# Input weights from transposes of a weighed table, and a rewritten start-up, in a state-space convolution with routed low-rank FFN

## The reference

```python
dtA = A * dt[:, None];  Cs = Cc * (jnp.exp(dtA) - 1.0) / A
P = dtA[:, :, None] * jnp.arange(length)
K = 2.0 * jnp.einsum('hn,hnl->hl', Cs, jnp.exp(P)).real
y = irfft(rfft(u * mask) * rfft(K)) [:L] + (u * mask) * D;  y = y * mask
logits = einsum('bsd,ed->bse', y, route_w);  topk_v, topk_idx = top_k(logits, 1)
route_weight = one_hot(topk_idx) * topk_v
h = einsum('bsd,erd->bser', y, A);  wh = route_weight[..., None] * h
out = x + einsum('bser,eor->bso', wh, Bw)
```

## Time and profile before

| | |
|---|---|
| three runs | 608.71, 609.56, 609.94 us (median 609.56) |
| the profiled execution | 609.9 us, its span 608.1 us |
| granted TensorE clock | 1.00 over the span |
| busy: PE, DVE, ACT, POOL | 581.6, 490.3, 317.2, 385.9 us |
| instructions in the span | 13318 |

### The profile page before, as it was taken

The page is one execution under the profiler, slowest core; times in us unless marked ns, Lnnn a source line. Parts: engine busy times, 40 slices in busy tenths (PEclk is TensorE's granted clock), DMA queues, the critical chain, the costliest instruction groups (busy, mean ns, idle before and its releaser), DMA issues.

```text
span 608.1 us, 13318 instructions
## 1 busy us (share of the span) xinstructions
PE 581.6 (96%) x3617; PEld 529.0 (87%) x3617; DVE 490.3 (81%) x1371; ACT 317.2 (52%) x1059; POOL 385.9 (63%) x520
## 2 busy tenths in 40 slices
PE   3589999999999999999999999999999999999996
PEld 3478999999999989999999999999999999999984
DVE  7768888887888888788888888888888888887875
ACT  3666754555465455546545554664555456445420
POOL 4668657666765766676575667657566765665430
PEclk9999999999999999999999999999999999999999
DMA  6212454454345344434534443453444345445422
GB/s 119 73 54 86 149 155 98 144 155 125 120 148 156 100 141 153 125 119 148 157 96 143 153 135 110 148 157 97 143 152 132 114 147 157 102 139 151 138 85 83
DMA packets 37582, 77.64 MB, mean 128 GB/s; under 512 B 12476, under 2 KB 20862, under 8 KB 37510
## 3 DMA queue, kind: packets, MB, share of 16 engines
q1 hardware_dynamic: 28358, 43.76, 28.8%
q10 hardware_dynamic: 9152, 33.03, 13.3%
HBM read 43.16 MB, written 33.62 MB: 126 GB/s over the span
## 4 chain that ended last, share of the span: by engine, by line
PE 92%; DVE 3%; ACT 2%; issue 1%; POOL 1%; DMA 0%; ACTq 0%; POOLq 0%
PE psYo L1060 20%; PE psZ L1080 19%; PE psO L1060 15%; PE psYe L1060 13%; PE psS L1060 11%; PE psO L1107 5%; PE psXe L1071 5%; PE psXo L1071 5%; PE psZ L1136 1%; DVE psS L918 0%; DVE ex L758 0%; DMA logs<-in_L_cond_log_dt_dram 0%; POOL both L465 0%; DVE ost L957 0%; ACT L577 0%
## 5 line engine op out<-in xcount | busy, mean ns | idle before, releaser
L504 POOL TENSOR_TENSOR Slo<-Sf,Shi 128x384 fp32r<-128x384 f32 x64 | 65.3, 1021 | 166.1 <-ACT Shi L651 166.1
L918 DVE SCALAR_TENSOR_TENSOR psS<-Sf,tab,psS 64x128 f32<-64x128 f32 x256 | 91.9, 359 | 48.1 <-ACT Sf L646 41.2
L1080 PE MATMUL psZ<-Wt,Y 128*128 128x136 f32 x1024 | 129.2, 279 | 0.0
L1080 PEld LDWEIGHTS psZ<-Wt,Y 128*128 128x128 f32 x1024 | 123.3, 190 | 0.1
L646 ACT ACTIVATE Sf<-psS 128x128 f32<-128x128 f32 x64 | 17.8, 277 | 200.3 <-PE psS L1060 200.3
L957 DVE TENSOR_TENSOR ost<-psO,xt 128x512 f32<-128x512 f32 x128 | 87.7, 690 | 1.2 <-PE psO L1060 1.1
L497 POOL TENSOR_TENSOR Xlo<-xeven,Xhi 128x512 fp32r<-128x512 f32 x64 | 82.9, 1295 | 0.0
L465 POOL TENSOR_TENSOR both<-coarse,fine 128x512 f32<-128x512 f32 x64 | 69.0, 1079 | 1.3 <-ACT fine L591 1.2
L941 DVE TENSOR_TENSOR wlo<-psZ,whi 128x128 fp32r<-128x128 f32 x64 | 18.7, 292 | 41.2 <-ACT whi L656 41.2
L1060 PE MATMUL psYo<-Xhi,Thi 128*128 128x512 f32 x128 | 51.2, 400 | 0.0
L1060 PE MATMUL psYo<-Xlo,Thi 128*128 128x512 f32 x128 | 51.1, 399 | 0.0
(11 more groups left out here) (193 smaller groups left out, 1522.2 us busy)
## 6 DMA issues: line engine op xcount, KB each, us to landing
xt<-in_x_dram SPq DMA_DIRECT2D x64, 512.0 KB, 4.9
out_dram<-ost ACTq DMA_DIRECT2D x63, 512.0 KB, 5.1
Traw<-kdram SPq DMA_DIRECT2D x64, 128.0 KB, 2.9
kdram<-krow SPq DMA_DIRECT2D x64, 1.0 KB
A_nat<-in_L_ffn_A_dram SPq DMA_DIRECT2D x1, 512.0 KB, 5.1
B_nat<-in_L_ffn_Bw_dram SPq DMA_DIRECT2D x8, 64.0 KB, 3.5
out_dram<-ost SPq DMA_DIRECT2D x2, 256.0 KB, 2.0
lens_i<-in_itok_B_dram SPq DMA_DIRECT2D x1, 64.0 KB, 5.0
```

The source lines that it names most:

```text
L504: pool.tensor_tensor(Slo[h.s2][:, :], Sf[h.s2][:, :], Shi[h.s2][:, :].bitcast(F32), ALU.subtract).then_inc(slo_done, 1)
L918: dve.scalar_tensor_tensor(psS[to, new], Sf[h.s2][fr, old], tab2[fr, BR, h.n:h.n + 1], psS[to, new], ALU.mult, ALU.add).then_inc(brought_d ...
L1080: last = pe.matmul(psZ[:, 0:NW], Y[:, j, c, :], Wt[:, 2 * c + j, :], start=(j == 0 and c == 0), stop=(j == 1 and c == NE - 1), skip_group_ ...
```

## The change

The matrix `Mx` and the constant `twin` go. Instead ACT weighs the table itself: `same` is Grev times the column MA of `tab2`, on all 128 partitions, and `cross` is Grev times MB, each half of 64 partitions read from the other half (`cross_parts`). POOL adds the two to `Wg` (`w_table`), and PE turns `Wg` by two transposes into psB. The samples of K come from a row sum of psB that ACT accumulates while it copies (`scrap`, twice), and K(0) with D folded in comes from a fifth column `K0` of the table.

```diff
-            def m_matrix(h):
-                need(act, b_mm, h.n - 1)
-                for j, table in enumerate((M0, M1)):
-                    act.activation(Mx[h.s2][:, j * N:(j + 1) * N], twin[:, j * N:(j + 1) * N], ACT.Copy,
-                                   scale=col(tab2[:, table, :], h)).then_inc(mx_done, 1)
-                act.activation(Mx[h.s2][:, P:P + 1], col(tab2[:, CK, :], h), ACT.Copy).then_inc(mx_done, 1)
+            def cross_parts(h):
+                need(act, grev_done, h.n + 1)
+                need(act, wg_done, h.n)
+                act.activation(same[:, :], Grev[h.s2][:, :], ACT.Copy, scale=col(tab2[:, MA, :], h)).then_inc(crossed, 1)
+                for to, fr in ((slice(0, N), slice(N, P)), (slice(N, P), slice(0, N))):
+                    act.activation(cross[to, :], Grev[h.s2][fr, :], ACT.Copy,
+                                   scale=tab2[fr, MB, h.n:h.n + 1]).then_inc(crossed, 1)
...
-                act.activation(kcol[h.s2][:, 0, 0:1], psB[:, 0, P:P + 1], ACT.Copy).then_inc(kcol_done, 1)
-                act.activation(kcol[h.s2][:, 1, 0:1], psB[:, 1, P:P + 1], ACT.Identity,
-                               bias=Dcol[:, h.n:h.n + 1]).then_inc(kcol_done, 1)
+                need(act, kcol_done, h.n * 3)
+                for j in range(2):
+                    act.activation(scrap[:, j, :], psB[:, j, 0:N], ACT.Copy,
+                                   accum_out=kcol[h.s2][:, j, 0:1]).then_inc(kcol_done, 1)
+                act.activation(kcol[h.s2][:, 2, 0:1], col(tab2[:, K0, :], h), ACT.Copy).then_inc(kcol_done, 1)
...
+            def w_table(h):
+                need(pool, crossed, h.n * 3 + 3)
+                need(pool, b_mm, h.n - 1)
+                pool.tensor_tensor(Wg[h.s2][:, :], same[:, :], cross[:, :], ALU.add).then_inc(wg_done, 1)
...
-                    last = pe.matmul(psB[:, j, :], Grev[h.s2][:, j * P:(j + 1) * P],
-                                     Mx[h.s2][:, :], start=True, stop=True, skip_group_check=True)
+                    last = pe.transpose(psB[:, j, :], Wg[h.s2][:, j * P:(j + 1) * P], ident[:, :])
```

```diff
             def step(head):
...
-                if head(3).there:
-                    m_matrix(head(3))
                 if head(1).there:
                     x_hi(head(1), 0)
                     x_hi(head(1), 1)
+                if is_head(head(0), 1):
+                    b_hi(head(1))
                 if head(2).there:
                     b_hi(head(2))
...
                 if head(3).there and not is_head(head(0), 1):
                     g_hi(head(3))
+                    cross_parts(head(3))
+                if head(-1).there:
+                    w_hi(head(-1))
                 if part_at(head(7)):
                     turns(part_at(head(7)))
                 if part_at(head(4)):
                     mirror(part_at(head(4)))
-                if head(-1).there:
-                    w_hi(head(-1))
-                if head(3).there and is_head(head(0), 1):
+                if is_head(head(0), 1):
+                    mirror(parts[1])
+                    g_hi(head(2))
                     g_hi(head(3))
+                    cross_parts(head(3))
```

```diff
+            def keep_busy(bank_, n):
+                for _ in range(n):
+                    pe.matmul(bank_[:, 0:P], ident[:, :], ident[:, :], start=True, stop=True, skip_group_check=True)
...
+            keep_busy(psO[0], 7)
             inputs(first[0])
+            pe.wait_ge(tab_done, 2)
+            keep_busy(psS, 3)
             bring(first[0])
             turn_x(first[1], 0)
             turn_x(first[1], 1)
             inputs(first[1])
+            pe.wait_ge(blo_set, 2)
+            keep_busy(psY[0], 8)
+            from_states(first[0])
             within(first[0], 0)
             within(first[0], 1)
-            inputs(first[2])
-            from_states(first[0])
             run_steps(step)
```

More of the change, by code:

```diff
@@ L525, in step @@
                     g_lo(head(3))
+                    w_table(head(3))
             first = [Head(n) for n in range(4)]
-            exponents(pool, *RHO_PARTS[0])
             angle_steps(parts[0])
-            x_lo(first[0])
+            angle_steps(parts[1])
             turn_parts(parts[0])
@@ L709, in _, with b_high @@
             mirror(parts[0])
-            act.wait_ge(tabs_turned, 2)
-            act.activation(tab2[:, :, :], psX[0][:, 0:5 * H].rearrange("p (t h) -> p t h", h=H),
-                           ACT.Copy).then_inc(tab_done, 1)
-            act.wait_ge(tab_done, 2)
-            m_matrix(first[0])
-            for j in range(2):
+            def b_high(j):
                 act.wait_ge(b_turned, j + 1)
@@ L726, in _ @@
             b_hi(first[1])
+            s_hi(first[0])
+            x_even(first[1])
+            g_hi(first[1])
             t_hi(first[0])
-            s_hi(first[0])
-            g_hi(first[1])
-            x_even(first[1])
-            turns(parts[1])
-            m_matrix(first[2])
-            b_hi(first[2])
-            g_hi(first[2])
-            sines(parts[1])
-            m_matrix(first[3])
-            t_hi(first[1])
-            g_hi(first[3])
-            mirror(parts[1])
+            sines(parts[1])
+            cross_parts(first[2])
+            t_hi(first[1])
+            g_hi(first[2])
+            cross_parts(first[3])
             run_steps(step)
@@ L964, in step @@
                     x_lo(head(1))
+                if is_head(head(0), 1):
+                    turn_k(head(1))
+                    b_lo(head(1))
                 if head(-1).there:
@@ L1157, in step @@
                     turn_x(head(1), 1)
-                if head(2).there:
+                if is_head(head(0), 1):
+                    inputs(head(1))
+                elif head(2).there:
                     inputs(head(2))
@@ L1161, in step @@
                     project(head(-1))
+                if is_head(head(0), 1):
+                    inputs(head(2))
                 if head(0).there:
```

337 lines of the change are left out of this document (185 added, 152 removed).

## The result

The changed kernel takes 652.10 us (median of 4 runs, 651.65 to 652.22), the kernel before 609.14 us beside it. The ratio is 1.070 (95% interval 1.069 to 1.072). I had forecast 631.6 us and a range up to 641. The direction and the mechanism were right; two terms of the sum were too small, and one was missing. The profiled span is 650.4 us, 42.3 more than before.

What follows compares the result with a forecast made beforehand. PE bounds the kernel before, with ACT's chain 0.15 us behind; the change makes that chain the bound. Span 608.1 + 3.9 (start-up) + 18.6 (58 steps) - 0.5 (end) = 630.1; predicted time 631.6 us, range 612 to 641.

Steps and rivals of the forecast that it cites:

- second to `whi` 0.49 - 0.10 = 0.39: ACT, each step: `whi` starts 0.39 us after the second `cross` starts, with the usual overlap back.
- the sum 1.72 us from `Ghi` to `whi`: ACT, each step: `same` and two `cross` put `whi` at t + 5.59, t being the step's first ACT copy.
- POOL's part: hidden: POOL, each step: `Wg` adds one 734 ns instruction, hidden because PE needs it only at the next step's input weights.
- The start-up's term: Steps before step 3: t (first ACT copy) of step 3 comes 3.9 us later; from 4 us gained to 7 lost.
- the end: Last steps: 0.5 us less, as they have no weighing any more and no two transposes on PE.
- PE's two transposes: PE, each step: the two new transposes take 0.22 us, in place of input weights taking 0.45 us.
- the 8.63 us that PE would need: PE, each step: its own work falls from 8.86 to 8.63 us; 13.3 us less if PE stayed the bound.
- the accumulating copies and `m_matrix`: ACT ahead of `Shi`: added copies hidden, removed `m_matrix` gives nothing back, as ACT waits 0.35 us for DVE there.
- The first: Rival, ACT: copies between halves overlap like any others, only the column costs; 617.6 us in all; chance 0.17.
- The second (faster): Rival: the three ACT instructions take 0.93 us, PE stays the bound; 599.7 us, at best 592; chance 0.14.
- The third (`Shi` late): Rival, ACT: accumulating copies take so long that `Shi` is 0.2 us late or more; 643 us; chance 0.09.
- The fourth: Rival, start-up: the fillers don't raise PE's clock, which moves the time by nothing; no chance given.

Runs made afterwards that it cites:

- experiment 3: Two runs of the changed kernel: each `cross` writing the half it reads (wrong results), 642.44 us; the two `cross` instructions in swapped order, 643.80 us.
- Experiment 2: Kernel before, with `same` and two `cross` computed and thrown away behind `Ghi`, and `whi` behind them, ahead of `turns` and `mirror`: 638.17 us, ratio 1.048.
- Experiment 5: Changed kernel with the work the change had put into step 1 moved back ahead of it on all engines; steps unchanged: 642.67 us, ratio 1.055.
- last run of experiment 9: Changed kernel with only ACT's issue of the output's store moved from ahead of `Sf` to behind `Bhi`: 644.68 us, ratio 1.058.

## Why the prediction was wrong

**The step that failed first** was "second to `whi` 0.49 - 0.10 = 0.39", with the sum 1.72 us from `Ghi` to `whi`. The three instructions take 1.90 us. `Ghi` to `same` (0.31), `same` to `cross` and `cross` to `cross` (0.51 forecast, 0.52 and 0.53) were right in number, though not for the reason that I gave: without the crossing of the halves they are as far apart (experiment 3). The last one to `whi` is 0.53. I took the overlap from the four copies of a mirror, whose last one writes partitions 0 to 63; the last `cross` writes 64 to 127. Swapping the two brought it back (experiment 3). This is 0.14 us a step, and with 0.03 of rounding and of copies a little longer, 0.16 to 0.17, over 58 steps 9.4 us.

**A term that was missing** is the fourth step. "POOL's part: hidden" was true of `Wg` for PE, but `Wg` moves `Grev` 0.7 us on, under which DVE's `frac` is held, ahead of the carry. With the chain through ACT as bound, this costs 0.27 to 0.28 us in 13 steps, 3.6 us. Experiment 2, with the same chain and no `Wg`, doesn't have it. So the 58 steps are 18.6 + 9.4 + 3.6 = 31.6; measured 31.6.

**The start-up's term** was 3.9 us and is 10.2. t of step 1 is 43.50 and not 41.9: the first input weights start at 24.90 and not near 23.5, head 0's `Slo` at 31.37 and not near 30, and the rest is as long as I said (ACT's 2.59 us of waiting for the table of head 3 was in it). Step 1 takes 15.9 us and not 13.5; step 2 takes 11.6 and not 9.2. Three things weren't in my account. `Traw` of head 2 can't come before its samples are written to DRAM, and `krow` is made behind step 1's carry: `Thi` waits 2.38 us for the DMA, with `whi` behind it. POOL's `Grev` of head 4 takes 1.45 instead of 0.73 us, beside DVE's `rho` (55.44 to 56.89), exponents that the change had put there; it ends 0.58 us after it. And PE, waiting 3.62 us in step 2, then does the projection at the lower clock, 1.8 us longer. Experiment 5 shows that the order of the work around step 1 makes 9.05 us of it; how much each of the three is by itself wasn't measured.

**The whole miss.** The span is 650.4 us where I had 630.1. Of the 20.3 between, to the rounding, 9.4 are the overlap behind the last `cross`, 3.6 the fourth steps, 6.3 the start-up and 0.9 the end, where I had 0.5 less and there are 0.4 more. The cause of that last part is open; the stretch behind step 61's copy is 33.6 to 34.1 us in kernels that end alike.

**What was right:** PE's two transposes at 0.22 us, and the 8.63 us that PE would need (8.634 measured once nothing else stood in the way); the accumulating copies and `m_matrix` at nothing; `whi` to `up` at 0.70; the 2.89 us from `up` to the next t, though 0.16 of them were a wait behind the store that I hadn't seen (last run of experiment 9); 97 us of busy time for `same` and `cross` where I said 94. That ScalarE's chain, at 52% busy, takes the bound over from an engine at 96% was the whole of the forecast, and experiment 2 shows it by itself.

**The rivals.** The first, overlap as usual, fell: there was less overlap than I took, not more. With it falls, for these three, the rule that the prediction names from the Trainium skill ("ScalarE: Activation LUTs", section "What ACT_TABLE_LOAD costs"), that back-to-back ACTIVATEs overlap by about 93 ns; `same` behind `Ghi` keeps it (0.31 us behind a copy of 0.41). The second (faster) would have needed `whi` at t + 5.13; it isn't the instructions' price that can bring it, but their place: with `whi` ahead of them it is at t + 4.99. I had priced the edit at the place where it was put, which was right for the forecast, but had not asked if the place was needed. The third (`Shi` late) was wrong, it still waits 0.37. The fourth was wrong in its letter, since the fillers do speed TensorE up and step 3 comes 1.4 us earlier with them, and right in its account of next to nothing.

My range left too little room above. I had bounded the three instructions at 2.2 us from above, which would have been 58 x 0.47 = 27 us more, and then took only 9.4 us above the forecast into the range; and the start-up's "7 lost" was less than the 10.2 it became.

## What to carry to other kernels

Where the slack of a second chain is 0.15 us, ask of each added instruction whether what waits for it is on that chain, and put what is on it first: the same instructions cost 38 us ahead of `whi`, and behind it the ordinary step is back at PE's own length. Behind an instruction that is removed from the bound there is always a next one; here it was DVE's work held by GpSimd, then `wh`, then a store's issue, and the long fourth steps went only when all were out of the way (605.2 to 597.3 us, with another start-up in it). A DMA issue waits in order like any other instruction, so it stands where its engine idles and not ahead of the copy that a chain hangs on.

## What the hardware did that I hadn't expected

- ScalarE: the copy behind one that wrote partitions 64 to 127 starts 0.53 us behind its start, behind one that wrote 0 to 63 0.42 (experiment 3 against the changed kernel; the half that is written last is what both of its kernels change).
- VectorE beside GpSimd: a clamp of 128 x 128 takes 0.64 us instead of 0.23, and two products 0.78 to 0.92 instead of 0.35, in which the held one ends within 0.1 us of GpSimd's instruction. It goes the other way too: GpSimd's `Grev` took 1.45 us instead of 0.73 beside VectorE's `rho`.
- A copy with a row sum is two instructions in the trace, the second one `ACTIVATION_READ_ACCUMULATOR` with 0.21 us of its own, 128 of them; the pair takes about 0.2 us from start to start.
- TensorE's granted clock fell to its lower level (0.50) in idle times of 5.5 and 3.6 us in the start-up and was still there behind them, and 16 matmuls took 3.83 instead of 2.02 us.
